# One key projection for two heads in an attention and feed-forward kernel on Trainium2

## What is computed

```python
kv_r = _apply_rope(kv_c, sin_k[None], cos_k[None])
q_r = jnp.einsum('bshq,hqr->bhsr', q_big, W_qr)      # r = 64
k_r = jnp.einsum('bld,hdr->bhlr', kv_r, W_kr)        # r = 64
scores = jnp.einsum('bhsr,bhlr->bhsl', q_r, k_r)
attn = jax.nn.softmax(scores, axis=-1)
ctx_c = jnp.einsum('bhsl,bld->bhsd', attn, kv_r)
```

## Time and profile before

| | |
|---|---|
| three executions | 984.38, 985.65, 986.23 us; median 985.65 |
| the profiled execution | 986.32 us, of which the span of the trace is 984.5 us |
| busy share of the span | PE 89%, DVE 85%, ACT 50%, POOL 52% |
| one period of the loop | 46.98 us |
| heads 1 to 14 | some 658 us of the 984.5 (14 periods) |

### The profile page before, as it was taken

How to read it: one execution, slowest core, us unless ns; L and a number is a source line. 1 busy time by engine, 2 the same in 40 slices (tenths; PEclk the granted TensorE clock), 3 DMA queues, 4 the chain that set the end, 5 groups by cost and what they waited for, 6 DMA issues and landing times. The chain is left out here.

```text
span 984.5 us, 15195 instructions
## 1 busy us (share of the span) xinstructions
PE 879.4 (89%) x4381; PEld 685.6 (70%) x4390; DVE 838.0 (85%) x1232; ACT 489.3 (50%) x801; POOL 514.8 (52%) x543
## 2 busy tenths in 40 slices
PE   3649999999999999999999999999999776149996
PEld 3437888888888888888888888888888654014443
DVE  6659898989898889999898989898989566979995
ACT  2225455445454545555554545455545587774432
POOL 5277565656565556464646556565656103605541
PEclk9779999999999999999999999999999899559998
DMA  7000000000000101000000000000000650400000
GB/s 272 0 25 25 14 25 14 26 14 24 13 24 13 26 14 30 19 21 16 24 13 24 13 24 24 13 24 13 24 13 24 239 201 4 178 0 12 21 22 32
DMA packets 18262, 38.35 MB, mean 39 GB/s; under 512 B 1600, under 2 KB 8000, under 8 KB 16960
## 3 DMA queue, kind: packets, MB, share of 16 engines
q1 hardware_dynamic: 17152, 35.99, 11.0%
q10 hardware_dynamic: 1088, 2.10, 0.6%
HBM read 35.98 MB, written 2.10 MB: 39 GB/s over the span
## 5 line engine op out<-in xcount | busy, mean ns | idle before, releaser
L664 ACT ACTIVATE probs<-scores,neg_max 128x1024 f32<-128x1024 f32 x128 | 144.1, 1126 | 141.3 <-DVE neg_max L778 140.2
L655 ACT CAST pt_hi<-banks 128x512 fp32r<-128x512 f32 x256 | 144.7, 595 | 126.4 <-PE banks L920 126.4
L745 DVE TENSOR_TENSOR pt_lo<-banks,pt_hi 128x512 fp32r<-128x512 f32 x256 | 169.4, 683 | 20.0 <-ACT pt_hi L655 19.8
L575 POOL TENSOR_TENSOR rot_cos<-rot_cos,rot_sin 128x512 f32<-128x512 f32 x93 | 120.2, 1293 | 117.0 <-DVE rot_sin L754 106.1
L778 DVE TENSOR_REDUCE neg_max<-scores 128x1 f32<-128x1024 f32 x128 | 155.7, 1218 | 1.0
L920 PE MATMUL banks<-ident,probs 128*128 128x128 f32 x1024 | 143.9, 274 | 6.6 <-DVE rot_sin L754 2.3
L920 PEld LDWEIGHTS banks<-ident,probs 128*128 128x128 f32 x1024 | 123.4, 141 | 33.6 <-DVE acc L773 2.8
L583 POOL TENSOR_TENSOR rot_lo<-rot_cos,rot_hi 128x512 fp32r<-128x512 f32 x93 | 119.8, 1288 | 7.8
L937 PE MATMUL scores<-kr_hi,qr 128*128 128x512 f32 x256 | 109.1, 426 | 9.2 <-PEq L983 5.1
L937 PE MATMUL scores<-kr_lo,qr 128*128 128x512 f32 x256 | 102.1, 399 | 0.0
L855 PE MATMUL banks<-pt_hi,v_hi 128*128 128x512 f32 x256 | 100.6, 393 | 1.6 <-DVE pt_lo L745 1.6
(11 more groups left out here) (176 smaller groups left out, 1913.6 us busy)
## 6 DMA issues: line engine op xcount, KB each, us to landing
load<-in_pack SPq DMA_DIRECT2D x15, 320.0 KB, 2.9
load<-in_pack SPq DMA_DIRECT2D x16, 256.0 KB, 2.7
raw_early<-in_gate_w SPq DMA_DIRECT2D x4, 1024.0 KB, 8.1
raw_early<-in_val_w SPq DMA_DIRECT2D x4, 1024.0 KB, 15.9
load<-in_pack SPq DMA_DIRECT2D x16, 192.0 KB, 2.4
acc<-in_x ACTq DMA_DIRECT2D x4, 512.0 KB, 7.6
load<-in_pack SPq DMA_DIRECT2D x16, 128.0 KB, 2.1
raw_early<-in_out_w SPq DMA_DIRECT2D x2, 1024.0 KB, 22.2
```

The lines of the kernel that those rows point to most:

```text
L575: nc.gpsimd.tensor_tensor(total, total, rot_sin[:, c, :], ALU.add).then_inc(rot_sum, 1)
L655: nc.scalar.copy(out, src).then_inc(group_hi, 1)
L664: nc.scalar.activation(probs[:, u % 2, :], scores[:, u % 2, :], ACT.Exp, bias=neg_max[:, u:u + 1], accum_out=sums[:, u:u + 1]).then_inc(ex ...
L745: return nc.vector.tensor_tensor(pair[1], src, pair[0].bitcast(F32), ALU.subtract)
```

## The change

The weight of K now holds three slices of 64 columns: this pair's even head, its odd head, and the even head again. One group of three matmuls makes the keys of both heads for 512 positions: the columns 0 to 127 for the first half (even keys in the upper partitions 0 to 63, odd keys in 64 to 127), the columns 64 to 191 for the second half (odd above, even below). So K1x stands only in the periods of even heads, and K0x only in those of odd heads, and a period has two K groups where it had four.

What moves out of PSUM is stacked: there is a tile for each head, `kr_even` and `kr_odd`, with one part of the keys in one half of the partitions and the other part in the other half. ACT makes two copies of 64 partitions for a K group, DVE two subtractions of 64 partitions, of which each writes to the other half of the partitions than it reads from. The queries are two tiles, `qr_hi` and `qr_lo`, each with the same 64 rows twice. For that ACT copies C twice, and copies the low part once more, 64x512, when DVE has made it ("double").

Other edits come with it. `q` has no tile of its own any more and shares that of `cv`, and for that the group O13 moves from behind B10 to ahead of the second part of A1. The pair's slices come by three small DMAs into a tile `wk_raw` of their own. The order of banks is worked out for even and odd periods apart.

```diff
-    ("exp", 0), ("exp", 1), part(1, 2, V1), ("T", 0, 0), ("K", 1, 0),
+    ("exp", 0), ("double", 1, "last"), ("exp", 1), part(1, 2, V1), ("T", 0, 0), ("K", 1, 0),
...
-    ("score", 3), ("max", 3), ("K", 1, 1), ("T", 1, 1), ("O", 1, 2, "last"), part(1, 2, A1), ("T", 2, 0),
-    ("T", 2, 1), ("exp", 3),
-    ("score", 4), ("B", 1, 0, "next"), ("O", 1, 3, "last"), ("T", 3, 0), part(0, 3, C0), part(1, 3, C0),
+    ("score", 3), ("max", 3), ("K", 1, 1), ("T", 1, 1), ("O", 1, 2, "last"), ("O", 1, 3, "last"), part(1, 2, A1),
+    ("T", 2, 0), ("T", 2, 1), ("exp", 3),
+    ("score", 4), ("B", 1, 0, "next"), ("T", 3, 0), part(0, 3, C0), part(1, 3, C0),
...
-    ("score", 6), ("exp", 5), part(0, 8, V0), part(1, 8, V0), part(2, 8, V0), part(3, 8, V0), ("max", 6),
+    ("score", 6), ("exp", 5), ("double", 0, "next"), part(0, 8, V0), part(1, 8, V0), part(2, 8, V0), part(3, 8, V0), ("max", 6),
...
+        if group[0] == "K" and (group[1] == 0) != odd:
+            return False
...
-        split(h, 3, [w[:] for w in t["wk"]], twice(src, CQ * R, 1)).then_inc(wk_ready, 1)
+
+    def key_pair(h):
+        pool.wait_ge(t["pair_loaded"], h.pairs(48))
+        pool.nop(nofuse=True)
+        nc.gpsimd.tensor_scalar(t["wk"][0][:], t["wk_raw"][:], 1.0, 0.0, ALU.mult, ALU.add).then_inc(t["pair_hi"], 1)
+        pool.wait_ge(t["pair_hi"], h.pairs(1))
+        nc.gpsimd.tensor_tensor(t["wk"][1][:], t["wk_raw"][:], t["wk"][0][:].bitcast(F32), ALU.subtract).then_inc(wk_ready, 1)
...
+        def keys_at(group):
+
+            _, b, half = group
+            one, other = (x[:, b, half * 512:(half + 1) * 512] for x in (kr[half], kr[1 - half]))
+            return (slice(0, R), one), (slice(R, 2 * R), other)
...
+                for n, head in enumerate((h, h.plus(1), h)):
+                    src = pack[bass.ds(head.after(4, WRK), 1), :, CQ * R:CQ * R + R].rearrange("o p n -> (o p) n")
+                    sp.dma_start(t["wk_raw"][:, n * R:(n + 1) * R], src).then_inc(t["pair_loaded"], 16)
...
-                pool.wait_ge(group_full, p.full(("K", 1, 1)))
+                pool.wait_ge(group_full, p.full(("T", 1, 1)))
...
-                    out, src = qr[0:R, group[1], :], banks[0:R, p.bank[marked], :]
+                    src = banks[0:R, p.bank[marked], :]
+                    nc.scalar.copy(qr[0][0:R, group[1], :], src)
+                    out = qr[0][R:2 * R, group[1], :]
                 elif kind == "K":
-                    out = kr[0][:, group[1], group[2] * 512:(group[2] + 1) * 512]
+                    (up, into_up), (down, into_down) = keys_at(group)
+                    nc.scalar.copy(into_up[up], banks[up, p.bank[marked], :])
+                    out, src = into_down[down], banks[down, p.bank[marked], :]
...
+                nc.scalar.copy(qr[1][0:R, b, :], qr[1][R:2 * R, b, :]).then_inc(doubled, 1)
...
+                    if kind == "K":
+                        (up, into_up), (down, into_down) = keys_at(group)
+                        nc.vector.tensor_tensor(into_up[down], banks[up, bank, :], into_up[up].bitcast(F32), ALU.subtract)
+                        return nc.vector.tensor_tensor(into_down[up], banks[down, bank, :], into_down[down].bitcast(F32),
+                                                       ALU.subtract)
...
-                                              qr[:, b, j * P:(j + 1) * P],
-                                              kr[low][:, b, half * 512:(half + 1) * 512],
+                                              qr[low][:, b, j * P:(j + 1) * P],
+                                              kr[odd][:, b, half * 512:(half + 1) * 512],
```

More of the change, by code:

```diff
@@ L64 @@
 A0, A1, V1, V0, C0, C1 = ("A", 0, "next"), ("A", 1, "next"), ("V", 1, "last"), ("V", 0), ("C", 0, "next"), ("C", 1, "next")
-UNGROUPED = ("score", "max", "exp", "sum")
+UNGROUPED = ("score", "max", "exp", "sum", "double")
 SCHEDULE = (
@@ L167, in __init__ @@
         else:
-            self.schedule = schedule_of(self.first, self.last)
-            self.order, self.bank = order_of(self.schedule), BANK
+            odd = head.number % 2
+            self.schedule = schedule_of(odd, self.first, self.last)
+            self.order, self.bank = order_of(self.schedule), BANK[odd]
             if self.first:
@@ L173, in __init__ @@
             else:
-                self.before = [(g, BANK[g]) for g in ALL]
+                self.before = [(g, BANK[1 - odd][g]) for g in ALL[1 - odd]]
                 self.start = head.after(GROUPS, GROUPS_BEFORE)
@@ L600, in prepare @@
                 first_split(WRK, start.first_loaded[WRK])
+                splits[PAIR](p.head)
                 rotate_here(0, 2, None)
@@ L655, in high_part, with double @@
                 nc.scalar.copy(out, src).then_inc(group_hi, 1)
+            def double(p, marked):
+                b = marked[1]
+                done = p.earlier(("C", b, "next")) if marked[-1] == "last" else p.place(("C", *marked[1:]))
+                act.wait_ge(group_read, p.read(done))
+                nc.scalar.copy(qr[1][0:R, b, :], qr[1][R:2 * R, b, :]).then_inc(doubled, 1)
             def exponentials(p, u):
@@ L892, in products @@
                 elif kind == "K":
-                    pe.wait_ge(wk_ready, h.after(1, 1))
+                    pe.wait_ge(wk_ready, h.pairs(1))
                     at = group[1] * L + group[2] * 512
-                    mm = three(out, [w[:, 0].rearrange("p o r -> p (o r)") for w in wk],
+                    mm = three(out, [w[:, group[2] * R:(group[2] + 2) * R] for w in wk],
                                [t[x][:, at:at + 512] for x in ("kt_hi", "kt_lo")])
@@ L929, in score_tile @@
                 b, j = divmod(u, U)
-                if b:
-                    queries = p.place(("C", 1)) if p.first else p.earlier(C1)
-                    pe.wait_ge(group_read, p.read(p.place(("K", 1, 1)), queries))
-                else:
-                    pe.wait_ge(group_read, p.read(p.earlier(("K", 0, 1, "next")), p.earlier(C0)))
+                odd = p.head.number % 2
+                if not odd:
+                    pe.wait_ge(group_read, p.read(p.place(("K", 1, 1)) if b else p.earlier(("K", 0, 1, "next"))))
+                pe.wait_ge(doubled, p.head.after(B, b + 1))
                 for half in range(2):
```

89 lines of the change are left out of this document (54 added, 35 removed).

## The result

The changed kernel took 1009.13 us (median of four executions, 1006.99 to 1010.94) beside 985.07 for the kernel before in the same comparison: ratio 1.0242, 95% interval 1.0219 to 1.0266. In a later comparison it took 1010.9 beside 984.61 (ratio 1.0253, 1.0207 to 1.030). The forecast was 998.5 with a range of 984 to 1006. The sign and the mechanism were right; the size was not, and the time lies 3 us outside the range.

The account below looks back on a forecast made before the run. PE's matmuls were taken to bound the loop, just short of waiting for K groups' banks. New waits less removed matmuls gave +11.0 us over seven turns, +11.7 with the ends: 997.4, with restarts 998.5; range 984 to 1006.

Parts of the forecast that it names:

- What bounds the kernel, and the ring: In the loop: PE's matmuls set the speed, with next to no room in the ring of three banks.
- Rival 1: In the loop: PE is the bound and the waits are not there, giving 963.6 us; chance 0.12.
- The reading of a K group: At each K group: second ScalarE copy starts 0.48 us after the first, second VectorE subtraction 0.71 after the first.
- The five named waits: PE waits per pair of periods: T01 0.48 us, O13 1.65, O03 1.2, T30 0.5 twice.
- What costs nothing: Query copies, second copies of C0 and C1, shared tile, weight splits and small DMAs were to add no wait.
- the removal: Two K groups fewer in each of 16 periods, 0.69 us each: 1.38 us a period, 22.1 on PE alone.
- the sum: Even periods +1.25 us, odd +0.32, seven turns +11.0; with the ends +11.7, 997.4, with restarts 998.5.
- this restart: PE getting going after each of the five waits of a pair: 0.1 us, counted half.
- Ahead of the loop, head 0, the way out: Outside the loop: +0.8 us ahead of it, +1.3 in head 0, -1.4 in head 15.
- Rival 3, the clock: PE's granted clock falls after a wait such as O13's: +17 us on top, 1015; chance 0.06.
- the term of a pair of periods: One turn of the loop, an even and an odd period: slower by 1.57 us, seven times.

Follow-up runs that it names:

- s_fix2: s_new2 with one move, K00 behind C0's last part in place of ahead of A1's second part: 971.8 us, ratio 0.987.
- e_one_read: Changed kernel, but each K group read by one ScalarE copy and one VectorE subtraction of 128 partitions (keys not the right ones): 984.48 us, ratio 0.9993.
- e_o13_late: Changed kernel with O13 back behind B10, the queries in their own tile, and their sine table left out: 996.29 us, ratio 1.0102.
- s_o12: Changed kernel with one group moved, O12 ahead of K11 in place of behind T11: 998.87 us, ratio 1.0127.
- s_three: s_o12 with two more moves, T01 ahead of K10, and K01 with T60 ahead of C1's second part: 994.18 us, ratio 1.0074.
- s_new2: Changed kernel in a new order of groups, K10 and K11 within V1, K00 ahead of A1's second part, K01 ahead of V0: 1007.87 us, ratio 1.0222.
- b_two_reads: Kernel before, with only each K group's read made two ScalarE copies and two VectorE subtractions of 64 partitions: 1031.33 us, ratio 1.0469.

## Why the prediction was right in kind and short in size

**What bounds the kernel, and the ring.** Right. Rival 1 (963.6) is out: the waits are there in every turn, and with them taken away (`s_fix2`) the time goes down to 971.8, not to 963.6.

**The reading of a K group.** Right for VectorE: the two subtractions start 0.69 apart and the next instruction 0.73 behind the second, where 0.71 was taken. Slightly short for ScalarE: the second copy starts 0.59 behind the first, where 0.48 was taken from two copies that begin in the same partition, and the next copy 0.61 behind the second. That the K groups' waits still came out within 0.1 us (O13 0.07, O03 0.05 and T01 0.08 over) fits this term, 0.11 more on ScalarE and 0.02 less on VectorE.

**The five named waits.** Right, 4.35 against 4.33. `e_one_read`, `e_o13_late`, `s_o12` and `s_three` each take away or shorten the waits that they should and leave the others, within 0.1 us. The single waits are less exact than their sum: T30 was put too high by 0.09, twice a pair.

**"What costs nothing" and the removal.** Here the sum failed. A pair grew by 2.6, so the delays grew by 5.36 with the 2.76 of matmuls that are gone; 1.0 lies outside the five waits. PE's starts in the same turn of after show where (score 0, then A0; further down score 2, then O10):

```profile
306.07 0.40 PE L990 MATMUL scores<-kr_odd,qr_lo 128*128 128x512 f32 x1
306.50 0.49 PE L909 MATMUL banks<-x_hi,wq_hi 128*128 128x512 f32 x1
306.83 0.39 PE L909 MATMUL banks<-x_lo,wq_hi 128*128 128x512 f32 x1
...
319.84 0.40 PE L990 MATMUL scores<-kr_odd,qr_lo 128*128 128x512 f32 x1
320.27 0.50 PE L909 MATMUL banks<-m_hi,cv_hi 128*128 128x512 f32 x1
```

O10 starts 0.43 behind the score matmul in place of 0.23 in odd periods: it needs `cv_lo`, and K10, which used to stand between, is gone there. The subtraction that makes it ends at 320.21:

```profile
319.52 0.69 DVE L799 TENSOR_TENSOR cv_lo<-banks,cv_hi 128x512 fp32r<-128x512 f32 x1 [0.81 <-ACT cv_hi L696]
```

The removed work had been the cover of another wait, and the prediction counted it as a pure gain. A0 is 0.20 late (0.08 in the even period) in the bank of C1, whose second copy the prediction had put at nothing ("behind C1 comes only T61": but A0 follows in the same bank). VectorE waits for that copy before it can start its two instructions on C1, and ends at 306.36:

```profile
304.34 0.58 ACT L696 CAST qr_hi<-banks 64x512 fp32r<-64x512 f32 x1
...
304.95 0.68 DVE L782 TENSOR_TENSOR rest<-banks,qr_hi 64x512 f32<-64x512 f32 x1 [0.50 <-ACT qr_hi L696]
305.67 0.69 DVE L785 TENSOR_TENSOR qr_lo<-banks,rest 64x512 fp32r<-64x512 f32 x1
```

The last part of C1 is 0.13 late. Behind a wait at an O or A group the second matmul comes 0.33 to 0.35 after the first and not 0.23; behind one at a transpose the next group is 0.06 late. The prediction had this restart at 0.1, which is right for the first kind, but counted it half for five waits, while it comes at the small waits as well. Late starts outside the five add up to about 0.6 in this turn, and the restarts to 0.7, where the turn of before has some 0.25 of such; with the 4.35 that is the 5.4. These causes are read from the rows: no run takes the lateness of A0 or of O10 away alone, and in `e_one_read`, which leaves both causes in place, both still stand at 0.2.

The sum has a slip besides: half of 0.1 us for five waits in seven turns is 1.75, which on 997.4 gives 999.1, where the prediction has 998.5.

**Ahead of the loop, head 0, the way out.** +2.1 and +0.4 against +0.8 and +1.3: 2.5 together for 2.1, so that two errors cancel. About 1 us at the way out of the loop was not foreseen, and no run was made for it.

**Rival 3, the clock.** It does not hold for waits of 1.7 us in the loop. In the window of 305.0 to 401.6 us of after, a whole turn, the granted clock is 1.00:

```profile
305.00:401.60 96.60, 93.01 (x464) 74.90 (x463) 85.50 (x123) 53.01 (x94) 52.91 (x58) 1.00 0.07 20
```

With a wait of 3.35 us it is true in five of seven turns of `s_new2`. The Trainium skill (TensorE: Matmul & The Clock Gate, "A second HAM failure mode: psum-queue depth-cycling") warns of short idle times between groups; the ones here, with PE busy for 96% of the turn, did not set it off.

So the step that failed is the term of a pair of periods, +1.57 where it was +2.6, 7 us over the loop: "what costs nothing" put C1's second copy at nothing, "what is removed" took K10 as pure gain, and the restarts were counted half and for five waits only. The range's upper bound took 2.1 a pair, and so was short as well.

## What to carry to other kernels

Where groups go round a ring of PSUM banks, write down for each kind how long it takes from its first matmul until its bank is read, and how much TensorE work stands up to the next user of that bank; a change that makes a read longer needs its order looked at again before it is judged, and here that turned +2.5% into -1.3%. A removed group is also cover that is gone: ask which wait it stood ahead of. Sum the small delays (a second wait in the in-order reader, a restart of 0.1 us) in full, once for each wait: over a loop they were as large as a named wait.

## What the runs showed of the hardware

A VectorE instruction on 64 partitions takes as long as one on 128 (0.68 and 0.68 to 0.69 us for 512 columns out of PSUM), and the one behind it starts 0.69 to 0.73 us later if it uses another half of the partitions, against 0.61 between two of 128, whether it crosses to the other half (`kr_odd` to `kr_even` in after) or stays in its own (`b_two_reads`). The Trainium skill (VectorE: DVE Perf Modes, "Two Vector instructions with no wait between them") gives a model in which an instruction is held until the earlier ones have finished when its input or output starts in another quadrant of 32 partitions than the last one's, and these rows agree with it: 338.29 + 0.68 is 338.97, and the next starts at 338.98.

ScalarE shows the same, which I had not expected: of its copies of 512 columns, each 0.58 long, one that begins in the other half of the partitions starts 0.59 behind its predecessor (`kr_odd`, then `kr_even`, at 374.65 and 375.24), and one in the same half 0.48. A copy of 64 partitions in the same half as the one ahead starts 0.48 behind it too (`qr_hi` behind `pt_hi` in after), so that the width of the later copy does not matter. Two copies of 64 hold up the copy behind them until 1.20 after the first one's start, one of 128 until 0.48.

TensorE's granted clock fell to 0.50 behind five of the seven waits of 3.35 to 3.37 us in the loop of `s_new2`, for 3 to 5.5 us, and stayed at 1.00 behind the other two and through all waits of 1.72 and less in the loop of after. Where between them it begins to fall, and what tells the five from the two, was not found. Outside the loop shorter waits were followed by the low level as well: in head 0 of after PE waits 2.07 us for a K group and soon afterwards 0.79, and from 81.6 to 85.2 us the clock is 0.53.
